# Attention logits on one core: the relative half in four quarter tiles of the array, with the first norm's steps moved among logits and transposes

## The chip, the cores and the metric

The kernel runs on one core of a Trainium2 chip. The metric is the device time of one execution in microseconds (us), the median of three runs. TensorE is called PE, VectorE DVE, ScalarE ACT, GpSimd POOL and SyncE, which issues DMAs, SP, as in the profile.

## The reference

64 images become 64 patch tokens each by a linear layer, a class token and 128 text tokens are joined to them: L = 193 tokens of 128 channels. Then comes attention with group norms and relative position terms, and a mixture of experts with 8 experts of 512, both as residuals. What the change touches is the attention:

```
qkv = group_norm(layernorm(h) @ W_qkv)          # 8 heads; q, k of 8 channels, v of 16
rel_idx = arange(L)[:, None] - arange(L)[None, :] + (L - 1)
rpe = rel_emb[:, rel_idx]                       # rpe_q, rpe_k (8 rows each), rpe_v (16)
logits = einsum('bhdi,bhdj->bhij', q, k) \
       + einsum('bhdi,dij->bhij', q, rpe_k) + einsum('bhdi,dij->bhij', k, rpe_q)
attn = softmax(logits)
out = einsum('bhij,bhdj->bhdi', attn, v) + einsum('bhij,dij->bhdi', attn, rpe_v)
h = h + group_norm(out);  h = h + ffn(layernorm(h))
```

In the mixture each token's two best gates multiply its input, every expert's dense layer is computed for both, gelu is applied to each and the two are summed before the second layer.

## The kernel before, in words

A first phase (`patch_embed`) makes the patch tokens. Then `fused_block` works on pairs of batch items, 32 pairs; channels lie on the 128 partitions, the 2 x 193 = 386 tokens of a pair along the free side. Each engine has its own instruction stream, written by hand: all go through the same list `SCHEDULE`, and for each name in it every engine issues its part of that step, in order. Engines meet through counting semaphores. One passage of the list is a turn. In a turn the MLP of pair n (32 chunks `c` or `a`, one per 128 of the 4096 hidden units) alternates with the attention of pair n+1, and the names in `EARLY` belong to the first half of the attention of pair n+2 (`txt` to `gaff`). There are 30 such turns in a loop, one more behind it with no early part, one ahead of it without MLP and one at the end with MLP alone.

A chunk (`mlp`): PE makes z in three matmuls of 386 columns into one of two banks (L429, L430, L433), VectorE multiplies z by a ratio (L607), ScalarE applies gelu to z in the bank (L817) and to the product (L818), GpSimd adds both (L889, issued two chunks later), and PE multiplies by the second layer's weights three chunks later (L420). A chunk's z waits for the first gelu of the chunk two before it, since it reads the same bank.

The attention of a pair:
- `txt`, `mean1`, `var1`, `bc1`, `proj`: transposes of the text, first layer norm (matmuls with a matrix of ones for sums and broadcasts, vector operations between, a power on GpSimd), projection to q, k, v. `gmean`, `gvar`, `gaff`: group norm of q, k, v by small matmuls and operations on 4 elements per partition; three of them on VectorE (`group_affine`, L650 to L654), then four scalings on ScalarE (L837, L840).
- SP writes q and k to DRAM and reads them back 8 times over into `a_rep`. `am0` to `am3` on VectorE multiply `a_rep` by a mask into `a_bd` (L700); `qs0` to `qs4` on GpSimd multiply q by a mask into `q_bd` (L918). So both hold block diagonal weights for blocks ("octs") of 8 queries times 16 (item, head) pairs: 25 octs.
- `log0` to `log12`: two octs each. PE: q_bd with k (L517), then a_bd with the relative rows `rw` (L518), added in the same bank, 193 columns each. The contraction of L518 has 128 rows: 16 source rows times 8 queries. Every fp32 matmul call is two instructions in the trace. Four banks are used in turn. VectorE takes the maxima (L710), ScalarE the exp (L858) into `lp`.
- `tr0` to `tr6`: transposes of four octs each into two banks, copied by VectorE (L715) and ScalarE (L864). `rel0` to `rel6`: product with the relative rows of v (L561, L562), masked by VectorE into `wm`, which lies in lp (L723).
- `pv0`, `pv1`: products with v and with ones, four column tiles of 32 at once (L543); `rec0`, `rec1`: reciprocals (L659); `place0`, `place1`: the relative part added to the banks, in the same tiles (L571), then normalised and measured for the next group norm by VectorE (L732 to L737).
- `omean`, `ovar`, `oaff`, `oh2`, `mean2`, `var2`, `bc2`, `gate`, `gate2`, `bcast`: output group norm, residual (L750), second layer norm, gates.

## Time and profile before

| | us |
|---|---|
| median of 3 runs | 3425.13 (3424.44 to 3427.97) |
| profiled execution, its own time | 3423.42 |
| its span | 3421.6 |

| engine | busy us | share of span | instructions |
|---|---|---|---|
| PE (matmul) | 3200.4 | 94% | 21952 |
| DVE | 1981.0 | 58% | 4052 |
| ACT | 1832.8 | 54% | 3570 |
| POOL | 1447.1 | 42% | 1350 |

The busy times are those of one profiled execution. A share is an average over the span; what bounds a stage is read from the timeline of that stage, where a bracket behind a row gives how long the engine stood idle and which instruction released it. Matmuls are pipelined, so the times of two rows overlap, and the distance from start to start is what one costs. PE's granted clock is 0.99 of full speed in the mean of the span.

### The profile page before, as it was taken

Reading aid. Unit: us, or ns where it says so; the run is one execution under the profiler, and the core shown is the slowest. Engines: PE = TensorE matmul, PEld = TensorE weight load, DVE = VectorE, ACT = ScalarE, POOL = GpSimd, SP = SyncE. Lnnn points to the kernel's source line nnn. Section 1 sums busy time; section 2 is a strip of 40 time slices with the busy share of each in tenths; the row PEclk is TensorE's granted clock in tenths of the full one; section 3 lists DMA queues with packets and bytes.
Section 4 is the critical chain, followed back from the end, with each engine's and each line's share of the span. In section 5 each row is a group of like instructions: output and inputs, shape, how many; then the busy total and the mean of one; then the engine's idle time right before and its main releaser. Section 6 shows DMA issues by size and latency. Waiting matters only on the chain.

```text
span 3421.6 us, 65186 instructions
## 1 busy us (share of the span) xinstructions
PE 3200.4 (94%) x21952; PEld 2602.3 (76%) x21952; DVE 1981.0 (58%) x4052; ACT 1832.8 (54%) x3570; POOL 1447.1 (42%) x1350
## 2 busy tenths in 40 slices
PE   7977999999999999999999999999999999999998
PEld 5867777777777777777777777777777777777776
DVE  4644655566565556665555566655555666655554
ACT  4632555555555555555555555555555555555556
POOL 1010444455434444554444445544444555344446
PEclk9987999999999999999999999999999999999999
DMA  9961001111110011111101111111011111100110
GB/s 202 219 179 30 14 16 26 24 26 26 26 24 9 22 24 26 26 26 26 24 7 24 24 26 26 26 26 24 5 26 24 26 26 26 26 23 6 24 25 5
DMA packets 92174, 121.41 MB, mean 35 GB/s; under 512 B 8414, under 2 KB 86558, under 8 KB 87710
## 3 DMA queue, kind: packets, MB, share of 16 engines
q1 hardware_dynamic: 87714, 118.24, 14.9%
q10 hardware_dynamic: 4432, 2.79, 0.3%
q8 instruction: 17, 0.28, 0.0%
q14 instruction: 11, 0.09, 0.0%
HBM read 106.04 MB, written 14.97 MB: 35 GB/s over the span
## 4 chain that ended last, share of the span: by engine, by line
issue 39%; PE 25%; POOL 15%; DVE 9%; ACT 4%; DMA 0%; DVEq 0%; POOLq 0%; ACTq 0%; SPq 0%
POOL gelu L889 10%; PE bank L420 7%; POOL q_bd L918 4%; PE bank L461 4%; PE bank L429 3%; DVE gelu L607 3%; PE bank L433 2%; DVE dl L760 2%; PE bank L430 2%; ACT gelu L817 2%; DVE gst L650 1%; PE bank L493 1%; POOL rs L902 1%; ACT e L840 1%; PE bank L449 1%
## 5 line engine op out<-in xcount | busy, mean ns | idle before, releaser
L889 POOL TENSOR_TENSOR gelu<-gelu 128x386 f32<-128x386 f32 x1024 | 1068.3, 1055 | 1477.9 <-ACT gelu L818 1474.7
L817 ACT ACTIVATE gelu<-bank,b_s 128x386 f32<-128x386 f32 x1024 | 595.2, 581 | 878.2 <-DVE gelu L607 867.0
L420 PE MATMUL bank<-gelu,w_s 128*128 128x386 f32 x2048 | 834.8, 494 | 45.6 <-POOL gelu L889 41.4
L607 DVE TENSOR_TENSOR gelu<-bank,ratio 128x386 f32<-128x386 f32 x1024 | 565.1, 557 | 476.4 <-PE bank L433 470.7
L818 ACT ACTIVATE gelu<-gelu,b_s 128x386 f32<-128x386 f32 x1024 | 624.3, 610 | 0.0
L429 PE MATMUL bank<-x_hi,w_hi 128*128 128x386 f32 x1024 | 524.6, 512 | 78.0 <-ACT gelu L817 73.8
L420 PEld LDWEIGHTS bank<-gelu,w_s 128*128 128x128 f32 x2048 | 361.6, 189 | 105.6 <-POOL gelu L889 87.0
L517 PE MATMUL bank<-k_f,q_bd 128*128 128x193 f32 x1600 | 393.6, 328 | 8.2 <-DVE a_bd L700 8.2
L518 PE MATMUL bank<-rw,a_bd 128*128 128x193 f32 x1600 | 393.2, 328 | 0.0
L858 ACT ACTIVATE lp<-bank,mx 128x193 f32<-128x193 f32 x800 | 288.0, 419 | 195.5 <-DVE mx L710 194.3
L429 PEld LDWEIGHTS bank<-x_hi,w_hi 128*128 128x128 f32 x1024 | 193.9, 189 | 253.7 <-ACT gelu L817 176.6
L710 DVE TENSOR_REDUCE mx<-bank 128x2 f32<-128x386 f32 (+1 forms) x416 | 225.1, 541 | 259.8 <-PE bank L518 255.9
L433 PE MATMUL bank<-x_lo,w_hi 128*128 128x386 f32 x1024 | 347.2, 339 | 0.0
L430 PE MATMUL bank<-x_hi,w_lo 128*128 128x386 f32 x1024 | 347.1, 339 | 0.0
L561 PE MATMUL bank<-probs,rv 128*128 128x128 f32 x1600 | 309.1, 274 | 0.0
L562 PE MATMUL bank<-probs,rv 65*128 65x128 f32 x1600 | 309.1, 274 | 0.0
L723 DVE TENSOR_TENSOR lp<-bank,con 128x512 f32<-128x512 f32 (+1 forms) x224 | 139.0, 633 | 284.4 <-PE bank L562 284.4
L517 PEld LDWEIGHTS bank<-k_f,q_bd 128*128 128x128 f32 x1600 | 281.9, 191 | 8.6 <-issue 8.6
L518 PEld LDWEIGHTS bank<-rw,a_bd 128*128 128x128 f32 x1600 | 283.6, 191 | 0.0
L562 PEld LDWEIGHTS bank<-probs,rv 65*128 65x128 f32 x1600 | 242.2, 191 | 0.0
L561 PEld LDWEIGHTS bank<-probs,rv 128*128 128x128 f32 x1600 | 241.8, 191 | 0.0
L530 PE MATMUL bank<-con,lp 128*128 128x128 f32 (+1 forms) x1600 | 220.8, 275 | 17.6 <-ACT lp L858 10.5
(131 smaller groups left out, 4266.6 us busy)
## 6 DMA issues: line engine op xcount, KB each, us to landing
a_rep<-u_scratch SPq DMA_DIRECT2D x32, 1600.0 KB, 9.8
xt<-in_x SPq DMA_DIRECT2D x192, 196.0 KB
txt_s<-in_txt SPq DMA_DIRECT2D x32, 128.0 KB, 2.2
u_scratch<-k_f SPq DMA_DIRECT2D x32, 100.0 KB, 2.2
u_scratch<-q_f SPq DMA_DIRECT2D x32, 100.0 KB, 2.2
out<-o_s SPq DMA_DIRECT2D x64, 48.5 KB
out<-o_s SPq DMA_DIRECT2D x64, 48.0 KB
rv<-in_rel_v SPq DMA_DIRECT2D x1, 2624.0 KB, 14.0
```

The source lines that it names most:

```text
L420: mm(yb[:, 0:T2], w2_s[:, f, :], gelu1[:, f % RING, :], start=(f == 0), stop=(f == NF - 1)).then_inc(S["w2_done"], 1)
L429: mm(z, w1_hi[:, w], x_hi[:, :], start=True, stop=False)
L430: mm(z, w1_lo[:, w], x_hi[:, :], start=False, stop=False)
L433: mm(z, w1_hi[:, w], x_lo[:, :], start=False, stop=True).then_inc(S["z_ready"], 1)
L517: mm(dst, q_bd[:, o, :, :], k_f[:, 0:L], start=True, stop=False)
L518: m = mm(dst, a_bd[:, o, :, :], rw[:, 192 - 8 * o:192 - 8 * o + L], start=False, stop=True)
L561: mm(part, rv[:, (8 * o + P) * HD:(8 * o + P) * HD + P], pr[0][:, o, :, :], start=True, stop=False)
L562: m = mm(part, rv[0:JC[1][1], 8 * o * HD:8 * o * HD + P], pr[1][0:JC[1][1], o, :, :], start=False, stop=True)
L607: v.tensor_tensor(gelu2[:, f % RING, :], zb[f % 2][:, 0:T2], ratio[:, :], ALU.mult).then_inc(S["z2_done"], 1)
L817: a(gelu1[:, f % RING, :], zb[f % 2][:, 0:T2], ACT.Gelu, bias=b1_s[:, f:f + 1]).then_inc(S["g_done"], 1)
L818: a(gelu2[:, f % RING, :], gelu2[:, f % RING, :], ACT.Gelu, bias=b1_s[:, f:f + 1]).then_inc(S["g_done"], 1)
L889: g.tensor_tensor(gelu1[:, f % RING, :], gelu1[:, f % RING, :], gelu2[:, f % RING, :], ALU.add).then_inc(S["hs_done"], 1)
```

## The change

It has four parts.

1. The relative half of the logits. The mask blocks become groups of 4 queries: `q_bd`, `a_bd` and `probs` go from [P, 25, 16, 8] to [P, 50, 16, 4]. `a_rep` holds the 16 source rows 4 times in each half of the partitions, filled by two DMAs of half the size instead of one. For an oct o the two groups g of 4 queries are computed with 64 rows (partitions 0 to 63 for even o, 64 to 127 for odd o) and 64 columns (64 g), so that four such calls have four different quarters of the array. `rw` is laid out to match.
2. A logits step has four octs in two banks; two sets of two banks alternate, so there are 7 steps instead of 13, and PE waits for the exps of the step before last. Even octs go to the first bank of a set, odd ones to the second. The q half stays as it was in the array. The first transpose waits for the last but one step, whole.
3. Mask pieces: `AM` is (0, 6, 12, 20, 25) octs, `QS` (0, 4, 12, 20, 25), one piece fewer, and am1 and qs1 stand ahead of the first logits step, the others about two steps ahead of their use.
4. The order. The early steps of the next pair move: txt, mean1 and var1 between the logits steps, bc1 behind tr1, proj behind rel6, gmean, gvar and gaff among pv, place and their chunks. Three chunks `c` stand ahead of am0 instead of four, and six instead of seven ahead of the logits; another one stands between place0 and place1.

The rows of `lp` become 196 long instead of 193, `wm` keeps whole rows, and the mask for it has full rows. The diff, cut to its core:

```diff
-RW = 2 * L - 1
+RW = 2 * L + 3
...
 SCHEDULE = (
-    "c c c c am0 c qs0 c c vt hkeep log0 am1 log1 qs1 log2 am2 log3 qs2 log4 log5 am3 log6 qs3 log7 log8 "
-    "qs4 log9 log10 log11 log12 tr0 tr1 rel0 c tr2 rel1 c tr3 rel2 tr4 rel3 tr5 rel4 tr6 rel5 rel6 "
-    "c pv0 c rec0 pv1 c rec1 place0 txt place1 c c omean mean1 c ovar c var1 oaff c bc1 oh2 c proj mean2 c "
-    "gmean c var2 gvar c bc2 c gaff c gate c c gate2 c c c c bcast w2t xin w2t w2t ot a otr a ocopy hres a"
+    "c c c am0 c qs0 c am1 c vt qs1 hkeep log0 log1 am2 qs2 log2 am3 log3 qs3 txt log4 mean1 log5 var1 log6 "
+    "tr0 tr1 bc1 rel0 c tr2 rel1 c tr3 rel2 tr4 rel3 tr5 rel4 tr6 rel5 rel6 "
+    "proj c pv0 c rec0 gmean pv1 c rec1 gvar place0 c place1 gaff c c omean c ovar c c oaff c oh2 c mean2 c var2 c c "
+    "bc2 c gate c c gate2 c c c c bcast w2t xin w2t w2t ot a otr a ocopy hres a"
 ).split()
...
-FILLS = (OCT + 1) // 2
-QS = (0, 5, 10, 15, 20, OCT)
-AM = (0, 7, 13, 19, OCT)
-LOGS = 4
+LGRP = 4
+LOGS = (OCT + LGRP - 1) // LGRP
+QS = (0, 4, 12, 20, OCT)
+AM = (0, 6, 12, 20, OCT)
...
-        lp = sb("lp", [P, OCT, L])
-        pr = [sb(f"probs{c}", [P, OCT, BH, 8]) for c in range(2)]
+        lp = sb("lp", [P, OCT, 196])
+        pr = [sb(f"probs{c}", [P, 2 * OCT, BH, 4]) for c in range(2)]
...
-                sp.dma_start(a_rep[:, :, :], u_scratch[:, :, :, :].rearrange("s d b i -> (s d) (b i)").unsqueeze(1)
-                             .broadcast_to([2 * DK, 8, BH * LP])).then_inc(S["a_spread"], 16)
+                for half in range(2):
+                    sp.dma_start(a_rep[64 * half:64 * half + 64, :, :], u_scratch[:, :, :, :].rearrange("s d b i -> (s d) (b i)").unsqueeze(1)
+                                 .broadcast_to([2 * DK, 4, BH * LP])).then_inc(S["a_spread"], 16)
...
-                    if i >= LOGS:
-                        pe.wait_ge(S["log_done"], t * FILLS + i - LOGS + 1)
-                    for k in range(2 if 2 * i + 1 < OCT else 1):
-                        o = 2 * i + k
-                        dst = lt[(i + 2) % LOGS][:, k * 256:k * 256 + L]
-                        mm(dst, q_bd[:, o, :, :], k_f[:, 0:L], start=True, stop=False)
-                        m = mm(dst, a_bd[:, o, :, :], rw[:, 192 - 8 * o:192 - 8 * o + L], start=False, stop=True)
+                    if i >= 2:
+                        pe.wait_ge(S["log_done"], t * LOGS + i - 1)
+                    octs = range(LGRP * i, min(OCT, LGRP * i + LGRP))
+                    place = lambda o: lt[2 * ((i + 1) % 2) + o % 2][:, o // 2 % 2 * 256:o // 2 % 2 * 256 + L]
+                    for o in octs:
+                        mm(place(o), q_bd[:, 2 * o:2 * o + 2, :, :], k_f[:, 0:L], start=(o // 2 % 2 == 0), stop=False, skip_group_check=True)
+                    for o in octs:
+                        row = 64 * (o % 2)
+                        for g in range(2):
+                            x0 = 196 - 8 * o - 4 * g
+                            m = mm(place(o)[64 * g:64 * g + 64, :], a_bd[row:row + 64, 2 * o + g, :, :],
+                                   rw[row:row + 64, x0:x0 + L], start=False, stop=True, skip_group_check=True,
+                                   tile_position=(row, 64 * g))
                     m.then_inc(S["log_ready"], 1)
...
                         if g == 0:
-                            pe.wait_ge(S["log_done"], t * FILLS + FILLS - 2 + c)
+                            pe.wait_ge(S["log_done"], t * LOGS + LOGS - 1)
...
-                    v.tensor_tensor(a_bd[:, o0:o1, :, :],
-                                    a_rep[:, :, 8 * o0:8 * o1].rearrange("p b (o r) -> p o b r", r=8),
-                                    K["mask_q"].unsqueeze(1).unsqueeze(1).broadcast_to([P, o1 - o0, BH, 8]),
+                    v.tensor_tensor(a_bd[:, 2 * o0:2 * o1, :, :],
+                                    a_rep[:, :, 8 * o0:8 * o1].rearrange("p b (o r) -> p o b r", r=4),
+                                    K["mask_q"].unsqueeze(1).unsqueeze(1).broadcast_to([P, 2 * (o1 - o0), BH, 4]),
                                     ALU.mult).then_inc(S["a_masked"], 1)
...
-                    act.wait_ge(S["max_done"], t * FILLS + i + 1)
-                    for k in range(w):
-                        o = 2 * i + k
-                        m = a(lp[:, o, 0:L], lt[(i + 2) % LOGS][:, k * 256:k * 256 + L], ACT.Exp, bias=mx[:, o:o + 1])
+                    for k in range(2 if LGRP * i + 1 < OCT else 1):
+                        act.wait_ge(S["max_done"], t * (2 * LOGS - 1) + 2 * i + k + 1)
+                        for z in range(2 if LGRP * i + 2 < OCT else 1):
+                            o, col = LGRP * i + k + 2 * z, LGRP * i + 2 * k + z
+                            m = a(lp[:, o, 0:L], lt[2 * ((i + 1) % 2) + k][:, z * 256:z * 256 + L], ACT.Exp, bias=mx[:, col:col + 1])
                     m.then_inc(S["log_done"], 1)
```

## Rows read from the trace of the kernel before

**Rows 1.** Busy time of each engine by stage of one turn, 1510.7 to 1608.8, and sum.
```profile
core 0: us, PE busy (x) PEld busy (x) DVE busy (x) ACT busy (x) POOL busy (x), PEclk, DMA share, GB/s
...
1527.00:1543.40 16.40, 16.40 (x103) 16.38 (x102) 9.73 (x15) 10.42 (x28) 8.11 (x6) 1.00 0.00 0
...
sum 98.10, PE 93.37 PEld 75.53 DVE 57.99 ACT 53.50 POOL 44.98; mean PE 18.67 PEld 15.11 DVE 11.60 ACT 10.70 POOL 9.00
```

**Rows 2.** PE's timeline, logits and first transposes (start, us, engine, line, idle before).
```profile
1527.05 0.49 PE L517 MATMUL bank<-k_f,q_bd 128*128 128x193 f32 x2
...
1543.38 0.60 PE L530 MATMUL bank<-con,lp 128*128 128x128 f32 x4
1544.31 1.11 PE L530 MATMUL bank<-con,lp 128*65 128x128 f32 x8 [0.33 <-ACT lp L858]
1545.64 0.65 PE L530 MATMUL bank<-con,lp 128*65 128x128 f32 x4 [0.22 <-ACT probs L864]
```

**Rows 3.** PE's timeline, single places of the same turn.
```profile
1525.86 0.92 PE L420 MATMUL bank<-gelu,w_s 128*128 128x386 f32 x2 [0.77 <-POOL gelu L889]
...
1579.81 0.28 PE L580 MATMUL bank<-gst_o,con 128*128 128x2 f32 x2
...
1580.56 0.81 PE L420 MATMUL bank<-gelu,w_s 128*128 128x386 f32 x2
1581.20 0.77 PE L455 MATMUL bank<-con,e 128*97 128x1 f32 x8
...
1594.77 0.92 PE L420 MATMUL bank<-gelu,w_s 128*128 128x386 f32 x2 [0.27 <-POOL gelu L889]
...
1599.34 0.44 PE L429 MATMUL bank<-x_hi,w_hi 128*128 128x386 f32 x1 [0.60 <-ACT gelu L817]
```

**Rows 4.** PE's timeline, product with v in column tiles and its neighbours.
```profile
1570.93 0.52 PE L543 MATMUL bank<-probs,v_pad 65*32 65x200 f32 x8
1571.27 0.52 PE L543 MATMUL bank<-probs,one_pad 65*32 65x200 f32 x8
1571.72 0.44 PE L429 MATMUL bank<-x_hi,w_hi 128*128 128x386 f32 x1
...
1572.35 0.81 PE L420 MATMUL bank<-gelu,w_s 128*128 128x386 f32 x2
1573.09 0.94 PE L571 MATMUL bank<-lp,con 128*32 128x200 f32 x16
```

**Rows 5.** ScalarE's timeline of that turn.
```profile
1533.78 1.36 ACT L858 ACTIVATE lp<-bank,mx 128x193 f32<-128x193 f32 x4 [1.29 <-DVE mx L710]
...
1597.10 0.51 ACT L837 ACTIVATE q_f<-bank,gst 128x193 f32<-128x193 f32 x1 [0.88 <-DVE gst L654]
...
1598.70 0.59 ACT L817 ACTIVATE gelu<-bank,b_s 128x386 f32<-128x386 f32 x1
```

**Rows 6.** VectorE's timeline of that turn.
```profile
1531.65 1.63 DVE L700 TENSOR_TENSOR a_bd<-a_rep,con 128x768 f32<-128x768 f32 x1
...
1535.57 0.95 DVE L700 TENSOR_TENSOR a_bd<-a_rep,con 128x768 f32<-128x768 f32 x1
...
1541.62 0.56 DVE L710 TENSOR_REDUCE mx<-bank 128x2 f32<-128x386 f32 x1 [0.75 <-PE bank L518]
...
1544.02 0.69 DVE L715 COPY probs<-bank 128x512 f32<-128x512 f32 x1
...
1573.03 1.36 DVE L659 RECIPROCAL t<-bank 128x193 f32<-128x193 f32 x1
...
1575.04 0.18 DVE L737 BATCH_NORM_AGGREGATE mv_o<-st_o 128x2 f32<-128x6 f32 x1
...
1584.97 0.76 DVE L750 TENSOR_TENSOR h<-h,t 128x193 f32<-128x193 f32 x2
...
1595.01 1.66 DVE L650 TENSOR_TENSOR gst<-vec,gst 128x4 f32<-128x4 f32 x1
```

**Rows 7.** GpSimd's timeline of that turn.
```profile
1521.83 1.77 POOL L889 TENSOR_TENSOR gelu<-gelu 128x386 f32<-128x386 f32 x1 [0.16 <-ACT gelu L818]
1523.56 1.29 POOL L918 TENSOR_TENSOR q_bd<-q_f,con 128x640 f32<-128x640 f32 x1
...
1593.70 2.94 POOL L889 TENSOR_TENSOR gelu<-gelu 128x386 f32<-128x386 f32 x3
```

65 lines of the change are left out of this document (33 added, 32 removed).

## The prediction

> **What bounds the kernel now.** I first read the table of busy time by stage of one steady turn [rows 1]: TensorE (PE) works 93.4 of 98.1 us. The turn, in which MLP chunks and the attention of the next pair alternate, comes 31 times at nearly the same length, so the change is worth 31 times what it does to one turn. Then I read PE's timeline for the places where it stands still. The logits run from 1527.05 to 1543.38 without a gap, 50 calls of 0.327 us [rows 2]. Behind them PE stands 0.33 us for an exp and 0.22 us for a copy of transposed probabilities. Of its other stops three matter here: 0.77 us before the logits, because GpSimd's sum is late, and in the long second half 0.27 and 0.60 us [rows 3]. So PE's work counts in full, and anything that makes a small chain late shows at once.
>
> **PE work removed.** The relative half is 25 of the 50 calls, 25 x 0.327 = 8.17 us. After the change it is 50 calls of 64 rows by 64 columns, in the order (row 0, column 0), (0, 64), (64, 0), (64, 64): one round of four calls per two blocks of eight queries, 2 rounds in a full step of four blocks and 1 in the last, so 13. The trace has no row tiles. The nearest is the product with v in four column tiles: 8 instructions (four calls) start every 0.34 us with 200 columns [rows 4], where one call alone takes about that, so four streams go at once. Lower bound of a round: 0.327 + 0.01 = 0.33 us, if the two row halves run together as the columns do. Upper bound: only the column pair does, 0.66 us. I take 0.33, since the column case is the nearest row and even and odd blocks write different banks: 13 x 0.33 = 4.29, a gain of 3.88 us.
>
> **Changes of array mode.** Each step now goes from the full array to tiles and back. Two full-array instructions of the MLP are followed by the next full-array one after 0.64 us (1580.56 to 1581.20 [rows 3]), but by the tiled one after 0.74 us (1572.35 to 1573.09): 0.09 to 0.10 us to go in. The last tiled round starts at 1571.27 and would end its turn at 1571.61, the next full instruction starts at 1571.72: 0.11 us to come out [rows 4]. Seven steps x 0.20 = 1.41 us. Net PE work: -3.88 + 1.41 = -2.47 us per turn. Chunks, transposes, products with v and the first norm's own matmuls are the same in number. The one chunk now between place0 and place1 costs the same out and in as txt did there.
>
> **The logits' pipeline.** A step is 4 x 0.327 + 2 x 0.33 + 0.20 = 2.17 us for PE. Its two banks come free when VectorE has reduced the first (start 0.2 us after PE, 0.56 us [rows 6]) and ScalarE has done four exps (1.36 us [rows 5]): with two hand-overs of 0.03 to 0.06 us, 2.21 us after the step. The step after next waits for that, having had 2.17 us: 0.04 us, nothing. But the third mask piece (1024 elements) stands on VectorE between the reductions of steps 1 and 2. 768 elements took 0.95 us alone and 1.63 us beside GpSimd's work [rows 6], so it takes 1.2 to 2.1 us where about 1.1 are free; step 4 then waits 0 to 0.63 us. I take 0.35. The query spread has pieces of 4 and 8 blocks; by 1.29 us for 5 [rows 7], 8 take some 2.1 to 2.3, just inside step 0's 2.17 us. The fourth mask piece and the vector operations of txt and mean1 fit, because mean1's matmul (two instructions of 386 columns, 0.64) makes step 5 late anyway.
>
> **Into the transposes.** tr0 needs step 5's exps, 2.21 us after that step. In between PE has var1 (eight instructions, 0.77 with the overlap of the last [rows 3], 0.62 to the next start) and the last step (2 x 0.327/2 + 0.33 + 0.20 = 0.87): a stop of 0.72 us. The copy of tr0 on VectorE ends 0.2 + 0.69 us [rows 6] after tr0's first half, while PE has another 0.44 of work, tr0's second half: 0.50 more. Against 0.33 + 0.22 today [rows 2] that is +0.67 us. bc1 does not help, it comes behind tr1.
>
> **Ahead of the logits.** The mask piece am0 made a GpSimd sum take 1.77 us where three others take 2.94 together, and with the query piece (1.29) behind it gave PE's 0.77 us stop [rows 3, 7]. Now two mask pieces (0.95 each) stand there, but qs0 has 4 blocks and one chunk fewer is there. Bounds -0.2 (shorter qs0) and +0.5 (am1 holds GpSimd up as am0 does); I take +0.1.
>
> **The group norm's affine, moved to right behind place1.** This is the largest charge. I count from place0's start. rec1 on VectorE (1.36 us, started 0.06 us before place0 today [rows 6]; gvar's matmul makes that 0.2) ends at 1.1; gvar's small add follows, GpSimd's power lasts from 1.3 to 2.3, if it takes what a sum does; place0's three operations (0.83 us from the end of rec1 to 1575.22) end at 2.2, then chunk A's multiply. PE: place0 0.87, A till 2.15, place1 till 3.1, B (inputs of its multiply at 3.9) till 4.4, C till 5.6, omean, and at 5.7 it wants D, whose bank must have been read by B's first gelu. VectorE: place1's operations end at 4.1, then the affine's three small ones. A chunk is 1.28 us of PE (1571.72 to 1573.09 [rows 4] without the 0.09), its multiply's input is there 0.8 in. GpSimd, held at the power, then has the sums of three chunks without a pause, from 2.3 to 5.35. Today the first affine operation, four elements from SBUF with SBUF, lay on VectorE from 1595.01 to 1596.67 and ended with a row of three sums (1593.70 to 1596.64) [rows 6, 7]. If that repeats, the affine ends at 5.75; without it, at 4.65. ScalarE then does q, k and v (1597.10 to 1598.70 today, 1.6 us [rows 5]) ahead of B's gelu (0.59). D starts at 8.05 or 6.95: a stop of 2.35 or 1.25 us. I take 2.35, as that is what the row shows for this instruction in this situation. Today's 0.60 us stop has the same cause, and the 0.27 us is a late sum behind two powers, one of which moves [rows 3]: -0.87. Net +1.48, lower bound +0.38.
>
> The Trainium skill, "SBUF — State Buffer", section "Who interferes with whom", says that a VectorE instruction with two SBUF inputs contends with GpSimd's reads, and that the winner of the shared ports holds them for the whole instruction. The row agrees that there is contention, but the wait passed over the end of a sum at about 1595.7, so it was longer than one instruction. If the page's unit of one instruction held, the affine would be free at 4.36 and the stop would be about 1.4 us and the sum -0.4 per turn, 3412 us: inside rival 1, and its chance is part of that rival's.
>
> **The second norm's chain.** Between ovar and mean2 PE now has four chunks, some 4.8 us. Today the chain of small steps from ovar's matmul (1579.81 [rows 3]) to the end of the two additions (1585.73 [rows 6]) lasts 5.9 us, hidden under three chunks and the first norm's matmuls; part of it is waiting behind that norm's vector operations, which are gone. Bounds 0 and 1.1 us of waiting; I take 0.25. Before var2 one chunk (1.2) stands against two vector operations of 386 columns (0.56 each as the reduction of as many) and hand-overs: 0.15. In all 0.4, bounds 0.15 and 0.9. DMA: the replicated source goes in two halves of the same bytes, asked for earlier against a need only slightly earlier; nothing.
>
> **The sum.** -2.47 + 0.35 + 0.67 + 0.1 + 1.48 + 0.4 = +0.53 us per turn; x 31 = +16.4. The profiled span of 3421.6 becomes 3438.0; that execution took 3423.4 (1.8 more), and the median 3425.1 is another 1.7 higher: **3441 us**. With all lower bounds: -2.47 + 0 + 0.67 - 0.2 + 0.38 + 0.15 = -1.47, 3379 us. With all upper: +0.63 + 0.67 + 0.5 + 1.48 + 0.9 - 2.47 = +1.71, 3478 us.
>
> **Rivals.** (1) **The affine isn't held up**: faster. Only the 1.10 us changes: +0.53 - 1.10 = -0.57 per turn, 3407 us. It decides at the point where the affine ends before GpSimd's row of sums does (under about 5.2 us after place0). For it: today this operation began when a third sum was already queued, there the row of sums may end sooner; against it the 1.66 us [rows 6]. With a free mask piece and ahead part as well it is the 3379 above. (2) **The row halves don't run together.** Rounds of 0.66: +4.29, less the 0.35 that a longer step hides, +0.53: +4.5 per turn, 3563 us. For it: no row of this trace has row tiles. Against it: banks and partitions are kept apart just as the columns' are. The gain would then not exist at all, only the mode changes. (3) **Runs of four elements are read more slowly.** The probabilities are now laid out in runs of four instead of eight, read by the 16 rounds of 0.34 us of the products with v; at double time +5.4 and the sum's +0.53 per turn, 3609 us. Nothing in the trace shows such runs; runs of eight go at the full rate. (4) **It cancels**: chain waits take what the tiles give, 3425 us.
>
> **How the numbers follow.** Forecast case 0.37 (own range 3428 to 3478), rival 1 and its neighbours 0.38, cancelling 0.13, row halves 0.08, runs of four 0.04. A change below 0.2% (7 us) can't be told from none with this kernel. Faster 0.38, within 0.2% 0.13, slower 0.37 + 0.08 + 0.04 = 0.49. The range, from 3375 to 3490 us, leaves out the two expensive rivals (0.12) and a little on the fast side. As cases of both signs hold most of the chance, the likeliest one's own range is 3428 to 3478.
>
> **What would show it.** Right: the relative instructions start in clusters of four, one cluster every 0.17 us; logits with about 14 us of PE work; a stop before tr0 of 0.7 us; and a stop of over 2 us at the second chunk after place1, released by ScalarE's gelu, while the affine's first operation lies over a row of sums. Wrong: the relative instructions one after the other (rival 2), products with v over 0.34 us per round (rival 3), or a short affine (rival 1). The prediction fails most easily on the waits of the second half, which are worked out from an order of instructions, not read.

## The result, and the profile after

| | before | after |
|---|---|---|
| median | 3425.51 us (3424.44 to 3427.97) | 3477.51 us (3474.60 to 3481.22) |
| span of the profiled execution | 3421.6 us | 3474.0 us |
| mean turn, from logits to logits | 98.07 us | 99.68 us |

The ratio is 1.0152, with a 95% interval of 1.0136 to 1.0168: the change makes the kernel slower by 52 us. The forecast was slower by 16 us, inside a range that went to 3490. The direction and most mechanisms hold; the size does not, and what follows is mostly about where the other 36 us lie. The medians are of all runs of a kernel and the ratios of its fast runs alone; the only slow run of this document is one of the four of e2_tiles (3512.5 us).

First, where in the span the 52.4 us between the two profiled executions are. From the first logits step on there are 31 turns. Thirty of them are longer by 1.61 us each: 48.3. The time up to the first logits step grows from 261.6 to 266.4 (+4.8), the first turn is shorter by 4.2, and what follows the last logits step is longer by 3.5. So the matter is decided in the steady turn. The table of busy time for a typical one of after (1546.12 to 1645.58; columns as in [rows 1]: stretch, length, busy time of PE, PE's weight loads, VectorE, ScalarE, GpSimd, each with its number of instructions, then granted clock, DMA share, GB/s):

```profile
1546.12:1645.58 99.46, 91.39 (x710) 70.89 (x709) 55.77 (x125) 53.32 (x110) 43.67 (x42) 1.00 0.09 23
```

PE is busy for 91.4 us of 99.5. Before, it was busy for 93.4 of 98.1 [rows 1]. PE's busy time has fallen by 2.0 us, as intended, and its idle time has risen by 3.3, from 4.7 to 8.1.

PE's timeline shows the logits (start, length, line, operation, tiles, count, and in brackets the idle time ahead of the row with what ended it). L519 is the q half in the full array, L524 the relative half in quarters; L451 is mean1, L457 var1, L538 the transposes, L422 and L431 chunks of the MLP:

```profile
1544.93 0.92 PE L422 MATMUL bank<-gelu,w_s 128*128 128x386 f32 x2 [1.25 <-POOL gelu L898]
1545.68 0.60 PE L471 MATMUL bank<-con,e 128*128 128x128 f32 x4
1546.12 1.47 PE L519 MATMUL bank<-k_f,q_bd 128*128 128x193 f32 x8
1547.52 0.89 PE L524 MATMUL bank<-rw,a_bd 64*64 64x193 f32 x16
1548.34 1.58 PE L519 MATMUL bank<-k_f,q_bd 128*128 128x193 f32 x8
1549.84 0.88 PE L524 MATMUL bank<-rw,a_bd 64*64 64x193 f32 x16
1550.65 1.57 PE L519 MATMUL bank<-k_f,q_bd 128*128 128x193 f32 x8
1552.16 0.89 PE L524 MATMUL bank<-rw,a_bd 64*64 64x193 f32 x16
1553.19 1.57 PE L519 MATMUL bank<-k_f,q_bd 128*128 128x193 f32 x8
...
1557.99 0.92 PE L451 MATMUL bank<-h,con 128*128 128x386 f32 x2
1558.74 1.47 PE L519 MATMUL bank<-k_f,q_bd 128*128 128x193 f32 x8
1560.14 0.88 PE L524 MATMUL bank<-rw,a_bd 64*64 64x193 f32 x16
1560.96 0.85 PE L457 MATMUL bank<-con,e 128*97 128x1 f32 x8
1561.67 0.57 PE L519 MATMUL bank<-k_f,q_bd 128*128 128x193 f32 x2
...
1563.10 1.09 PE L538 MATMUL bank<-con,lp 128*128 128x128 f32 x8 [0.39 <-ACT lp L867]
1564.54 1.09 PE L538 MATMUL bank<-con,lp 128*128 128x128 f32 x8 [0.35 <-DVE probs L724]
```

A full step is 2.31 to 2.32 us from start to start (1548.34 to 1550.65, 1547.52 to 1549.84), where 2.17 was forecast. The 16 instructions of its relative half start within 0.55 us in clusters of four, as this answer for a window of half a microsecond shows (duration least/median/most, then first and last start): twelve instructions of 0.32 us in a stretch of 0.4.

```profile
L524 PE MATMUL bank<-rw,a_bd x12: 322/323/375, 1547.5 to 1547.9; 64*64 64x193 f32 x12
```

So the quarters do run four at once. Without mean1 (0.75 us), var1 (0.71) and txt (0.28), which now stand between the steps, the logits take 14.85 us (1546.12 to 1562.71) against 16.33 before [rows 2]. That difference of 1.48 is not yet PE's work. The fourth step starts at 1553.19, which is 2.54 us after the third and 0.22 later than a full step would let it: it waited for the third mask piece on VectorE, which ends at 1552.96.

```profile
1551.74 1.22 DVE L708 TENSOR_TENSOR a_bd<-a_rep,con 128x1024 f32<-128x1024 f32 x1
```

And mean1, var1 and txt, each of which now stands behind a stretch of tiles, take some 0.1 us more here than behind full-array work (mean1 0.75 against the 0.64 that the prediction has for it), which is cost of the tiles too.

PE's stops in the second half of the turn, against 0.27, 0.60 [rows 3] and 1.04 us before:

```profile
1603.26 0.44 PE L431 MATMUL bank<-x_hi,w_hi 128*128 128x386 f32 x1 [1.97 <-ACT gelu L826]
...
1606.84 0.92 PE L422 MATMUL bank<-gelu,w_s 128*128 128x386 f32 x2 [0.21 <-POOL gelu L898]
...
1611.17 0.92 PE L451 MATMUL bank<-h,con 128*128 128x386 f32 x2 [1.06 <-DVE h L759]
...
1616.52 0.92 PE L422 MATMUL bank<-gelu,w_s 128*128 128x386 f32 x2 [0.53 <-POOL gelu L898]
```

A stop of 0.95 us follows at 1622.88, then 0.53, 0.27 and 1.25 ahead of the logits, as 0.54, 0.26, 0.25 and 0.76 before. The 1.97 is the forecast stop at the chunk called D in the prediction (the third whose z PE makes behind place1; the prediction's last paragraph and the expectations say the second), the 1.06 lies ahead of mean2, the others are late sums. The causes stand on VectorE (both affines: L658, L660, L662, which were L650 to L654) and on GpSimd (L911 a power, L898 the sums of chunks):

```profile
1599.58 0.23 DVE L658 TENSOR_TENSOR gst<-vec,gst 128x4 f32<-128x4 f32 x1
1599.84 0.94 DVE L660 TENSOR_TENSOR gst<-gst 128x4 f32<-128x4 f32 x1
1600.81 0.16 DVE L662 TENSOR_TENSOR gst<-vec,gst 128x4 f32<-128x4 f32 x1
...
1607.14 0.63 DVE L658 TENSOR_TENSOR gst_o<-vec,gst_o 128x2 f32<-128x2 f32 x1
1607.80 0.93 DVE L660 TENSOR_TENSOR gst_o<-gst_o 128x2 f32<-128x2 f32 x1
1608.77 0.93 DVE L662 TENSOR_TENSOR gst_o<-vec,gst_o 128x2 f32<-128x2 f32 x1
```

```profile
1597.81 2.95 POOL L898 TENSOR_TENSOR gelu<-gelu 128x386 f32<-128x386 f32 x3
1603.79 1.01 POOL L898 TENSOR_TENSOR gelu<-gelu 128x386 f32<-128x386 f32 x1 [3.03 <-ACT gelu L827]
1605.09 0.71 POOL L911 TENSOR_TENSOR gst_o<-gst_o,half 128x2 f32<-128x2 f32 x1 [0.29 <-DVE gst_o L751]
1605.77 3.92 POOL L898 TENSOR_TENSOR gelu<-gelu 128x386 f32<-128x386 f32 x4
```

An operation on two or four elements takes 0.16 us when GpSimd rests and up to 0.94 beside its sums. The reader should lay the two tables over each other: the row of three sums has its ends at about 1598.8, 1599.8 and 1600.8, and the first affine's operations end at 1599.81, 1600.78 and 1600.97. The row of four has ends at about 1606.8, 1607.7, 1608.7 and 1609.7, and the second affine's end at 1607.77, 1608.73 and 1609.70. Five of the six end within 0.02 us of a sum's end, and the next sum has started by the time the next operation does, so a chain of three can cost three sums. The sixth, the last of the first affine, begins when the row of sums is over and takes 0.16 us.

### The profile page after: what moved, and what is told of

It is laid out like the page before. It is cut to its first block, busy times and chain, and to the rows that moved or that the text cites. A ratio compares the mean times of both kernels' runs of the same rounds, so it can differ in the third digit from the quotient of the medians.

```text
span 3474.0 us, 67572 instructions
## 1 busy us (share of the span) xinstructions
PE 3158.1 (91%) x23552; PEld 2470.5 (71%) x23552; DVE 1891.3 (54%) x4052; ACT 1826.9 (53%) x3570; POOL 1409.5 (41%) x1318
## 4 chain that ended last, share of the span: by engine, by line
PE 52%; POOL 15%; issue 15%; DVE 6%; ACT 4%; POOLq 0%; DMA 0%; ACTq 0%; SPq 0%; DVEq 0%
POOL gelu L898 14%; PE bank L519 8%; PE bank L422 7%; PE bank L551 5%; PE bank L569 5%; PE bank L570 5%; PE bank L538 5%; PE bank L524 5%; PE bank L431 3%; PE bank L435 2%; PE bank L432 2%; PE bank L579 2%; PE bank L495 1%; ACT gelu L826 1%; PE bank L463 1%
## 5 line engine op out<-in xcount | busy, mean ns | idle before, releaser
L898 POOL TENSOR_TENSOR gelu<-gelu 128x386 f32<-128x386 f32 x1024 | 1057.4, 1048 | 1038.5 <-ACT gelu L827 1037.9
L422 PE MATMUL bank<-gelu,w_s 128*128 128x386 f32 x2048 | 848.3, 501 | 92.0 <-POOL gelu L898 88.2
L431 PE MATMUL bank<-x_hi,w_hi 128*128 128x386 f32 x1024 | 559.3, 546 | 88.1 <-ACT gelu L826 83.8
L422 PEld LDWEIGHTS bank<-gelu,w_s 128*128 128x128 f32 x2048 | 369.9, 192 | 156.3 <-POOL gelu L898 139.7
L867 ACT ACTIVATE lp<-bank,mx 128x193 f32<-128x193 f32 x800 | 274.1, 424 | 206.6 <-DVE mx L719 203.3
L431 PEld LDWEIGHTS bank<-x_hi,w_hi 128*128 128x128 f32 x1024 | 196.9, 192 | 252.7 <-ACT gelu L826 153.0
L719 DVE TENSOR_REDUCE mx<-bank 128x2 f32<-128x386 f32 (+1 forms) x416 | 208.5, 540 | 272.7 <-PE bank L524 272.7
L911 POOL TENSOR_TENSOR rs<-rs,half 97x4 f32<-97x4 f32 x64 | 65.1, 1017 | 656.6 <-DVE rs L638 656.6
L519 PE MATMUL bank<-k_f,q_bd 128*128 128x193 f32 x1600 | 312.3, 336 | 13.9 <-DVE a_bd L708 8.4
L519 PEld LDWEIGHTS bank<-k_f,q_bd 128*128 128x128 f32 x1600 | 259.1, 191 | 52.6 <-ACT lp L867 25.4
L432 PEld LDWEIGHTS bank<-x_hi,w_lo 128*128 128x128 f32 x1024 | 198.0, 193 | 70.3 <-issue 2.5
L873 ACT ACTIVATE probs<-bank 65x512 f32<-65x512 f32 (+1 forms) x224 | 121.6, 543 | 228.3 <-PE bank L538 228.3
```

Of the source, the lines that this page charges most:

```text
L422: mm(yb[:, 0:T2], w2_s[:, f, :], gelu1[:, f % RING, :], start=(f == 0), stop=(f == NF - 1)).then_inc(S["w2_done"], 1)
L431: mm(z, w1_hi[:, w], x_hi[:, :], start=True, stop=False)
L432: mm(z, w1_lo[:, w], x_hi[:, :], start=False, stop=False)
L519: mm(place(o), q_bd[:, 2 * o:2 * o + 2, :, :], k_f[:, 0:L], start=(o // 2 % 2 == 0), stop=False, skip_group_check=True)
L867: m = a(lp[:, o, 0:L], lt[2 * ((i + 1) % 2) + k][:, z * 256:z * 256 + L], ACT.Exp, bias=mx[:, col:col + 1])
L898: g.tensor_tensor(gelu1[:, f % RING, :], gelu1[:, f % RING, :], gelu2[:, f % RING, :], ALU.add).then_inc(S["hs_done"], 1)
```

## The experiments

All kernels here compute the whole of the reference. "Turn" is the mean distance between the logits of two turns, from the profile, with 98.07 for before and 99.68 for after. "Turn at full clock" is the mean of those turns in which PE's granted clock never falls to half, and behind it stands how many of the 30 turns in the loop have such a fall; it is 98.07 (0) for before and 99.47 (13) for after. The kernel before had medians of 3423.8 to 3424.9 us in the three groups of runs, and each ratio is to the one of its own group.

| kernel | median us | ratio (95%) | turn us | turn at full clock |
|---|---|---|---|---|
| e1_order: before + the new order | 3514.16 | 1.0262 (1.0244 to 1.0279) | 101.17 | 100.68 (19) |
| e2_tiles: after with the old order of the norm | 3462.32 | 1.0105 (1.0085 to 1.0125) | 98.98 | 98.76 (4) |
| e3_gaff: after, gaff behind bc2 | 3458.31 | 1.0107 (1.0090 to 1.0124) | 99.01 | 99.01 (0) |
| e4_modes: after, changes of mode doubled | 3540.35 | 1.0339 (1.0321 to 1.0356) | 101.72 | 101.41 (18) |
| e5_oaff_act: second affine on ScalarE | 3472.04 | 1.0141 (1.0124 to 1.0158) | 99.58 | 99.08 (10) |
| e6_am2: e2 + am2 ahead of the logits | 3435.43 | 1.0030 (1.0018 to 1.0043) | 98.25 | 98.08 (3) |
| e7_mix: tiles + a third order | 3407.35 | 0.9949 (0.9932 to 0.9965) | 97.50 | 97.50 (0) |
| e9_hold: after, GpSimd waits for the first affine | 3444.80 | 1.0057 (1.0040 to 1.0074) | 98.60 | 98.60 (0) |
| e8_qs0: e7 + qs0 a turn earlier | 3377.35 | 0.9858 (0.9842 to 0.9875) | 96.50 | 96.50 (0) |
| e10_qs01: e8 + qs1 too | 3364.48 | 0.9828 (0.9807 to 0.9850) | 96.03 | 96.03 (0) |
| e11_serial: after, quarter by quarter | 3482.59 | 1.0168 (1.0147 to 1.0188) | 99.81 | 99.62 (14) |

**The two halves of the change alone.** e1_order keeps the full array and takes the order:

```diff
-    "c c c c am0 c qs0 c c vt hkeep log0 am1 log1 ...
-    "c pv0 c rec0 pv1 c rec1 place0 txt place1 c c omean mean1 c ovar c var1 oaff c bc1 oh2 c proj mean2 c "
+    "c c c am0 c qs0 c am1 c vt qs1 hkeep log0 log1 log2 log3 am2 qs2 log4 log5 am3 log6 qs3 log7 txt qs4 "
+    "log8 log9 mean1 log10 log11 var1 log12 tr0 tr1 bc1 rel0 ... rel6 proj c pv0 c rec0 gmean pv1 c rec1 gvar "
+    "place0 c place1 gaff c c omean c ovar c c oaff c oh2 c mean2 c var2 c c bc2 c gate ..."
```

> The kernel before with the new order alone: logits still 13 steps on the full array, first norm's steps among logits and transposes, gaff behind place1, am1 and qs1 ahead of the logits. Theory A (the order costs, the tiles gain): PE keeps all 50 full calls, the second half has its stops of about 2 us at the second chunk after place1 and about 1 us before mean2; +2.5 to +3 us per turn against before, some 3505 to 3515 us. Theory B (the steps of four octs and the mode changes cost, the order is harmless): within 10 us of before, 3425 us.

e2_tiles is after with the norm's steps where before has them, and four chunks ahead of am0:

```diff
-    "rec1 gvar place0 c place1 gaff c c omean c ovar c c oaff c oh2 c mean2 c var2 c c bc2 c gate c "
+    "rec1 place0 txt place1 c c omean mean1 c ovar c var1 oaff c bc1 oh2 c proj mean2 c gmean c var2 gvar c bc2 c gaff c gate c "
```

> The changed kernel with the old order of the first norm (txt to gaff where they stood, seven chunks ahead of the logits); tiles, steps of four octs and mask pieces as changed. Theory A: PE work 1.5 us less per turn, 0.7 to 1 us of new waits at the transposes and ahead of the logits: -0.5 us per turn, about 3410 us. Theory B: slower than before, 3450 us or more.

The order alone costs 3.10 us per turn, and the tiles on top of it give back 1.49 (101.17 to 99.68). At full clock it is 2.62 and 1.21; the rest are turns in which the clock falls, which the order alone has more of. e1 shows after's stops one for one: 1.86 us for a gelu behind place1, 1.07 ahead of mean2, 0.52 and 0.96 for late sums. That much was as expected. With the old order, however, the tiles did not give a gain but cost 0.91 (0.69 at full clock), and the first theory of e2 fails. VectorE's and PE's timelines of e2 say why:

```profile
1556.58 2.11 DVE L708 TENSOR_TENSOR a_bd<-a_rep,con 128x1024 f32<-128x1024 f32 x1
```

```profile
1558.93 1.57 PE L519 MATMUL bank<-k_f,q_bd 128*128 128x193 f32 x8 [1.04 <-DVE a_bd L708]
1568.02 1.09 PE L538 MATMUL bank<-con,lp 128*128 128x128 f32 x8 [1.08 <-ACT lp L867]
```

The third mask piece lay beside two of GpSimd's sums and took 2.11 us, so the fourth step waited 1.04. And with nothing of the norm between the last steps, tr0 waits 1.08 us for the exps of the last but one step: PE had saved time that the pipeline behind it did not give.

**e6_am2** moves the third mask piece ahead of the logits:

```diff
-    "c c c c am0 c qs0 c am1 c vt qs1 hkeep log0 log1 am2 qs2 log2 am3 ...
+    "c c c c am0 c qs0 c am1 c vt am2 qs1 hkeep log0 log1 qs2 log2 am3 ...
```

> The kernel e2_tiles with one mask piece (am2) moved from behind log1 to ahead of the logits. Theory: its 2.11 us beside GpSimd's sums were the stop of 1.04 us at log3; the stop goes, at most 0.3 us comes back at log1 because GpSimd's query piece is held up instead: -0.7 us per turn, about 98.2 us per turn. Rival: the exps set the pace and a stop of the same size appears at another step; turn within 0.2 us of e2_tiles' 99.0.

As expected: the stop at the fourth step is gone, 0.35 us for a piece of q_bd comes at the second, and the turn is 98.25 (98.08 at full clock, as before). So with the old order the tiles are worth nothing even with that stop gone: of the PE time saved, tr0's stop takes 0.74 (1.07 for 0.33) and the stop ahead of the logits 0.5 (1.25 for 0.76).

**The largest stop.** e3_gaff takes gaff to behind bc2:

```diff
-    "... place0 c place1 gaff c c omean c ovar c c oaff c oh2 c mean2 c var2 c c bc2 c gate c "
+    "... place0 c place1 c c omean c ovar c c oaff c oh2 c mean2 c var2 c c bc2 gaff c gate c "
```

> The changed kernel with only gaff moved from behind place1 to behind bc2. Theory A: the stop of 1.97 us at the second chunk after place1 goes, a stop of about 0.6 us like the old one comes at the gate: -1.4 us per turn, about 3435 us. Rival: the stop only moves, because the output norm's chain is what is late: within 10 us of the changed kernel, 3477 us.

The 1.97 us stop goes, but the turn falls by 0.67 only where 1.4 was expected, and 0.20 of that is the clock. Up to mean2 PE is 1.8 us earlier in the turn than in after (mean2 63.3 us behind the first logits step instead of 65.1), and behind bc2 it loses 1.3 us again. The stop ahead of mean2 stays at 1.06, so gaff was not its cause; at bc2's end a late sum costs 0.43 and a gelu 0.24 where neither was, and the turns that were longer than the typical one are typical again. e9_hold leaves the order alone and keeps GpSimd away from the affine: at gaff GpSimd waits for its end before it takes further sums.

```diff
+                elif s == "gaff":
+                    pool.wait_ge(S["affine"], t + 1)
```

> The changed kernel with one more wait on GpSimd: the two sums behind gaff don't begin before VectorE's three small operations of the q, k, v affine are done. Theory C: these then take 0.5 us instead of 1.4, the stop of 1.97 us at the second chunk after place1 falls by 0.8 to 1.0, but the sums come later and PE stops 0.3 to 0.6 us at a product with a late sum: -0.3 us per turn, about 3465 us. Rival (no contention, the affine is late for its inputs): stop unchanged, and slower by the late sums, 3485 us.

```profile
1592.68 0.13 DVE L658 TENSOR_TENSOR gst<-vec,gst 128x4 f32<-128x4 f32 x1
1592.84 0.16 DVE L660 TENSOR_TENSOR gst<-gst 128x4 f32<-128x4 f32 x1
1593.04 0.16 DVE L662 TENSOR_TENSOR gst<-vec,gst 128x4 f32<-128x4 f32 x1
```

```profile
1594.41 0.92 PE L422 MATMUL bank<-gelu,w_s 128*128 128x386 f32 x2 [0.79 <-POOL gelu L898]
```

The three operations take 0.52 us from the first start to the last end instead of 1.39, PE's stop for the gelu is gone, and one of 0.79 for the delayed sum stands in its place, more than the 0.3 to 0.6 expected. The turn falls by 1.08 us (0.87 at full clock), where 0.3 was expected. This is the direct proof of what makes the first affine long: the same operations at the same place in the order, with GpSimd at rest, are short.

**The stop ahead of mean2.** e5_oaff_act computes the output norm's affine on ScalarE, which doesn't take part in the contention:

```diff
-                    group_affine(2, gst_o, S["orstd"], S["oaff_part"], S["oaffine"], ...)
+                    a(gst_o[:, 5, 0:2], gst_o[:, 4, 0:2], ACT.Identity, scale=OS).then_inc(S["oaff_part"], 1)
+                    ...
+                        a(gst_o[:, 2, b:b + 1], gst_o[:, 0, b:b + 1], ACT.Identity, scale=gst_o[:, 5, b:b + 1]).then_inc(S["oaff_part"], 1)
+                    ...
+                    a(gst_o[:, 6, 0:2], gst_o[:, 2, 0:2], ACT.Identity, bias=OB, scale=-1.0).then_inc(S["oaffine"], 1)
```

> The changed kernel with the output group norm's affine (three operations on two elements, which took 0.63, 0.93 and 0.93 us on VectorE beside a row of GpSimd's sums) done by four small operations of ScalarE instead, nothing else moved. Theory C (VectorE's small operations are held up by GpSimd's): the chain to mean2 gets some 1 to 1.5 us shorter, the stop of 1.06 us before mean2 falls under 0.3 us, -0.8 us per turn, about 3452 us. Rival (the chain is late because of the chunks queued in it): stop unchanged within 0.2 us, 3477 us, or more by the ScalarE time added.

A miss for the most part: the stop falls from 1.06 to 0.72, not below 0.3. ScalarE's timeline shows what is late now: the gelu of a chunk stands ahead of the affine until 1605.30, and its four instructions take 1.13 us by themselves.

```profile
1604.79 0.61 ACT L824 ACTIVATE gelu<-gelu,b_s 128x386 f32<-128x386 f32 x1
1605.30 0.28 ACT L874 ACTIVATE gst_o<-gst_o,vec 128x2 f32<-128x2 f32 x1
1605.62 0.48 ACT L877 ACTIVATE gst_o<-gst_o 128x1 f32<-128x1 f32 x2
1606.13 0.30 ACT L879 ACTIVATE gst_o<-gst_o,vec 128x2 f32<-128x2 f32 x1
```

The turn at full clock is 0.39 us shorter, which is about the 0.34 by which the stop fell; in the mean only 0.10 of it is left, since a turn in which the clock falls is 1.5 us longer here and 0.5 in after. So the contention is a part of that stop (0.34 us at least). The rest is, by the rows, a chain that needs some 6 us from ovar's matmul to h and has four chunks, 4.8 us, to hide under; no run separates that.

**The price of a change of mode.** e4_modes divides each step in two, with the q half and the relative half of two octs in turn; this makes six more times in and out per turn and changes nothing else:

```diff
-                    for o in octs:
-                        mm(place(o), q_bd[...] ...)
-                    for o in octs:
-                        ...
+                    for pair in (octs[0:2], octs[2:4]):
+                        for o in pair:
+                            mm(place(o), q_bd[...] ...)
+                        for o in pair:
+                            ...
```

> The changed kernel with each full logits step split into q of two octs, relative of two octs, twice: six more changes into tiles and back per turn, same matmuls. With the 0.36 us per pair of changes read from the changed kernel's trace (step 2.32 us against 2.61 us of the full array, two rounds of 0.33): +2.2 us per turn, some 3545 us. With the 0.20 us of the prediction: +1.2, some 3515 us. If a change costs nothing, 3477 us.

```profile
1576.40 0.56 PE L525 MATMUL bank<-rw,a_bd 64*64 64x193 f32 x8
1576.89 0.92 PE L520 MATMUL bank<-k_f,q_bd 128*128 128x193 f32 x4
1577.74 0.56 PE L525 MATMUL bank<-rw,a_bd 64*64 64x193 f32 x8
1578.23 0.92 PE L520 MATMUL bank<-k_f,q_bd 128*128 128x193 f32 x4
```

The turn grows by 2.04 us for six pairs of changes, 0.34 each, or by 1.94 at full clock, 0.32 each. The rows give nearly the same: two half steps of 1.34 us (1576.89 to 1578.23) against one of 2.32, 0.36. I had put 0.20.

**Do the quarters need an order?** e11_serial issues the calls of one column half before those of the other, two of the same quarter behind each other:

```diff
-                    for o in octs:
-                        row = 64 * (o % 2)
-                        for g in range(2):
+                    for g in range(2):
+                        for o in list(octs[0::2]) + list(octs[1::2]):
+                            row = 64 * (o % 2)
```

> The changed kernel with the relative calls of a step in another order of issue: the two calls of one quarter next to each other, then the next quarter; same calls, same changes of array mode. If PE starts calls strictly in the order of issue, a quarter's second call holds up the next quarter's first: a full step has about 13 instruction times of 0.163 us instead of 4, +1.4 us per full step, +8 to +9 us per turn, about 3740 us. If quarters have queues of their own, no change, 3477 us.

```profile
L524 PE MATMUL bank<-rw,a_bd x12: 323/323/374, 1551.1 to 1551.5; 64*64 64x193 f32 x12
```

The same twelve in 0.4 us, a turn of 99.81, 5 us in all above after, where a strict order of starts was expected to cost 8 to 9 us per turn. The order within a step matters by 0.14 us per turn at most: the second call of a quarter doesn't keep those of the other quarters from starting.

**Putting it together.** e7_mix takes the tiles, am2 ahead of the logits, and of the norm only what fills the gap ahead of tr0. txt, mean1, var1 and bc1 stay near logits and transposes; proj, gmean, gvar and gaff go back behind the output norm:

```diff
+    "c c c am0 c qs0 c am1 c vt am2 qs1 hkeep log0 log1 qs2 log2 am3 log3 qs3 log4 txt log5 mean1 log6 "
+    "tr0 var1 tr1 rel0 c tr2 bc1 rel1 c tr3 rel2 tr4 rel3 tr5 rel4 tr6 rel5 rel6 c pv0 c rec0 pv1 c rec1 "
+    "place0 place1 c c omean c ovar c c oaff c oh2 c proj mean2 c gmean c var2 gvar c bc2 c gaff c gate c "
```

> Tiles with an order chosen by the stops seen: am2 ahead of the logits, txt, mean1, var1 and bc1 in the stops around the transposes, proj to gaff where they stood before, one chunk ahead of the logits moved behind. Theory: the stops at tr0 (1.08) and tr1 (0.35) are filled by 1.3 us of work, no stop behind place1, some 0.5 us at mean2: 97.5 us per turn, about 3410 us. Rival: the second norm's chain takes it all back (1 us or more at mean2): 98.2 us per turn or more, no gain over the kernel before.

97.50 us as expected, and the first kernel that is faster than before, by 0.5%. Whether the old layout with this order would be as fast wasn't run, so what of this gain needs the tiles is open. Its largest stops are 1.24 ahead of the logits, for a sum behind a piece of q_bd, and 1.04 after gate. e8_qs0 takes the first piece of q_bd out of that place: its q is known since gaff of the turn before, so it goes ahead of that turn's output steps.

```diff
-EARLY = "txt mean1 var1 bc1 proj gmean gvar gaff".split()
+EARLY = "txt mean1 var1 bc1 proj gmean gvar gaff qs0".split()
-    "c c c am0 c qs0 c am1 c vt am2 qs1 hkeep log0 log1 ...
+    "c c c am0 c c am1 c vt am2 qs1 hkeep log0 log1 ...
-    "c gate2 c c c c bcast w2t xin w2t w2t ot a otr a ocopy hres a "
+    "c gate2 c c c c bcast w2t xin w2t w2t qs0 ot a otr a ocopy hres a "
...
                             pool.wait_ge(S["log_ready"], t * LOGS)
+                            pool.wait_ge(S["ffn_in"], t * 2)
```

> e7_mix with the first query piece (qs0, 1.04 us of GpSimd) done a turn earlier, behind the output matmuls of the MLP, where GpSimd stands still for about 4 us. Theory: the stop of 1.24 us ahead of the logits falls to 0.2 to 0.4 us, nothing comes back: 96.6 us per turn, about 3380 us. Rival: GpSimd's first sum of the new pair comes later by as much and the stop only moves to the first chunks: 97.5 us per turn as e7_mix, 3407 us.

e10_qs01 does the same with the second piece (`qs0 qs1` in both places).

> e8_qs0 with the second query piece (eight blocks, 2.0 us) moved there too. The stop of 0.36 us at log1 (GpSimd's piece late) goes; but 3.1 us of GpSimd now lie ahead of the first sum where 4 us less the wait for x_lo are free, so a stop of up to 0.8 us may come at the third or fourth chunk. Between -0.3 and +0.5 us per turn against e8_qs0.

e8's turn is 96.50, with the stop ahead of the logits gone; against the expectation something comes back, since the stop at the second step for q_bd grows from 0.36 to 0.85 us. e10 has neither and a turn of 96.03. That is 0.47 less than e8, more than the expected range of -0.3 to +0.5 had; the stop of up to 0.8 us at an early chunk is there, but has grown only from 0.25 to 0.53. Its table of busy time, with PE at 91.3 of 96.0, the same work as after's 91.4:

```profile
1500.40:1596.44 96.04, 91.26 (x711) 70.45 (x710) 59.66 (x126) 52.99 (x111) 44.74 (x42) 1.00 0.10 23
```

So e10 beats both kernels, 1.7% below before. Its qs pieces would help the old layout too, perhaps; that wasn't run, so the 1.7% is not a measure of the tiles.

## Why the prediction was right or wrong

Per turn the sum was +0.53 us; the typical turn is longer by 1.41 and the mean one by 1.61. By the steps of the prediction, the differences of starts in the two traces give the following. The first line leaves out the 0.22 us that the fourth step waited and counts with it the 0.1 us that txt, mean1 and var1 each take longer behind tiles:

| step | forecast | found | off by |
|---|---|---|---|
| PE work of the logits, with changes of mode | -2.47 | -1.4 | +1.05 |
| third mask piece | +0.35 | +0.2 | -0.15 |
| into the transposes | +0.67 | 0.0 | -0.67 |
| ahead of the logits | +0.1 | +0.35 | +0.25 |
| second half: gaff (1.48) and second norm (0.4) | +1.88 | +2.3 | +0.4 |
| sum | +0.53 | +1.4 | +0.87 |

**PE work: right mechanism, the mode term mis-sized.** The rounds of four quarters take 0.33 us, as taken from the column tiles [rows 4]; rival 2 (row halves one after the other) is out, and so is rival 3: the products with v still start a round every 0.34 us with runs of four elements. The step that failed is "seven steps x 0.20 = 1.41". It was read as the distance between the last instruction of one mode and the first of the other. The trace of after has that distance about as forecast, 0.09 in and 0.11 out. But the first instruction behind a change is itself slower: the first cluster of quarters lasts 0.21 us where the next take 0.165, and the first full instruction 0.27 where the next take 0.16. In all 0.36 by the rows and 0.34 by e4, 0.32 at full clock. So the term put at 1.41 us per turn measures 2.4 to 2.5. Seven times 0.15 is 1.05 us per turn, 33 us over the kernel, as much as nearly the whole of the missing 36; the errors of the other terms nearly cancel each other (-0.15, -0.67, +0.25, +0.4), which is luck. The distance from a stretch's first instruction in one mode to the same place in the next one is what had to be measured; the trace of before held it only for chunks beside place and pv [rows 4].

Of the missing 36 us some 26 are the typical turn's 0.87, some 6 the turns in which the clock falls and some 4 lie outside the thirty turns.

The Trainium skill says in "TensorEngine Tiling (Array Packing)", section "Key Properties", that a change of tiling mode drains TensorE. The runs agree in so far as a change in and out costs 0.32 to 0.36 us; that it is a drain they don't show. Its other sentence there, that tiles work independently of each other, is what e11's pace bears out.

**Third mask piece: right.** The fourth step waited 0.22 us for it, inside the bounds of 0 to 0.63. GpSimd's work on q_bd (5.04 us from 1545.80 to 1550.84) was done before the piece began, so it took 1.22 us from 1551.74, the lower end of "1.2 to 2.1". In e2, with another chunk ahead, the same piece met two sums and took 2.11, the upper end. The bounds were right and which of them holds is a matter of half a microsecond of alignment.

**Transposes.** The two stops were forecast as 0.72 + 0.50 and are 0.39 + 0.35, as stops 0.19 more than before's 0.33 + 0.22 [rows 2], and nothing from start to start. A likely reason, which no run here separates: the last steps, var1 and mean1 gave PE more work ahead of tr0 than I had counted, since each step has a dearer change of mode. A part of the error of the first line comes back here.

**Ahead of the logits.** +0.35 is inside the bounds of -0.2 and +0.5. The cause named for the upper one stands in the trace: a sum beside a mask piece takes 1.64 us, and the query piece comes before the next two sums (2.68). The stop is 1.25 us with one chunk fewer.

```profile
1540.55 1.64 POOL L898 TENSOR_TENSOR gelu<-gelu 128x386 f32<-128x386 f32 x1 [0.25 <-ACT gelu L827]
1542.16 1.04 POOL L927 TENSOR_TENSOR q_bd<-q_f,con 128x512 f32<-128x512 f32 x1
1543.17 2.68 POOL L898 TENSOR_TENSOR gelu<-gelu 128x386 f32<-128x386 f32 x2
```

**gaff behind place1: right.** The stop was forecast at 2.35 us, released by ScalarE's gelu, and is 1.97 with that releaser; the affine was to end 5.75 us after place0's start, and ends 1600.97 - 1595.53 = 5.44 after it, which accounts for most of the difference between the two stops. Rival 1 (the affine isn't held up) is out, and e9 shows the cause. How it is held up was put wrongly, however. I took one operation to be kept waiting by a whole row of sums, as 1.66 us in before seemed to say [rows 6]; here no operation waits longer than one sum, and it is the chain of three that waits several times. The Trainium skill, "SBUF — State Buffer", section "Who interferes with whom", gives the instruction as the unit of the lock. After's rows agree (0.94, 0.63, 0.93 and 0.93 us, each ending with a sum of 1.0). Before's 1.66 us still doesn't fit, and no run here explains it. The estimate that I made from that rule, a stop of 1.4, let only one operation be held up; the rule holds in after's rows and my use of it was wrong. With three sums in a row both readings give nearly the same end, so this term came out right partly by luck.

**Second norm's chain: mis-sized.** 0.25 us of waiting was forecast ahead of mean2 and 1.06 found, at the upper bound of 1.1. I argued that a part of the old 5.9 us was waiting behind the first norm and would go; but the second affine now lies beside a row of four sums and costs 2.56 us (1607.14 to 1609.70) by the very contention that I had charged to gaff. Before it took 1.30 us (1582.09 to 1583.39). How much of the stop this makes is shown only from below, 0.34 us by e5. The sum with all upper bounds was too low here as well: it took 0.9 for the whole of this term, whose first part alone had an upper bound of 1.1. I applied the reason to the operation that moved and not to the one that stayed while the sums around it moved. The late sums of 0.21 and 0.53 us are new, too, where I let the old 0.27 go.

**A loss that no step had.** Thirteen of after's turns are 0.3 to 1.4 us longer than the typical one. Each of them has one stretch in which PE's granted clock falls to half, beginning within 1.7 us of the end of the 1.97 us stop, and none of the other turns in the loop has one. Two stretches of such a turn, directly behind the 1.97 us stop (which ends at 1702.75); the third number from the right is the granted clock:

```profile
1703.70:1705.40 1.70, 1.70 (x8) 1.56 (x7) 0.60 (x2) 1.56 (x3) 1.39 (x3) 0.63 0.04 12
1705.40:1707.10 1.70, 1.70 (x5) 1.08 (x4) 0.56 (x1) 0.97 (x2) 1.70 (x2) 0.50 0.93 248
```

Half of full speed is the lower of the two levels, 1.2 GHz. The mean turn is 0.22 us above the typical one, some 7 us of the 52. With the stop gone (e3 and e9) no such turn is left: in e3 all but the first of the loop lie between 98.93 and 99.04 us. It isn't the length of 1.97 us that it takes. In e2 and e6 the clock falls behind the stop of 1.08 us ahead of tr0, in four and in three turns, and each of these is 1.6 us longer. A stretch of one in e2, whose stop ended at 2061.75:

```profile
2063.40:2065.10 1.70, 1.70 (x10) 1.70 (x10) 0.69 (x1) 0.07 (x1) 0.00 (x0) 0.50 0.00 0
```

Yet after's own stops of 1.06 and 1.25 us are never followed by such a fall. What decides in which turns the clock falls, these runs don't show.

**Outside the loop.** The 4.8 us up to the first logits step aren't settled: this part of the span, in which the images come in by DMA, took 261.6 us in before and 264.7 to 274.2 in the other kernels (274.2 in e2, 273.5 in e6, 266.8 in e10), and no run was made to tell what of that is the order and what the DMA.

**Chances and range.** 0.49 for slower was too modest a weight for what turned out clear, but the rivals on the fast side all leaned on the affine alone. The forecast's own upper sum was 3478 us, with every term at its upper end; the time came there by another road, one term (the mode) outside its bounds because it had none.

## What to carry to other kernels

Here small tiles would pay only for longer stretches in one mode: each time in and out costs 0.32 to 0.36 us with these fp32 calls, as much as one full-array call of 193 columns, so gather the calls of a mode before you divide the work. A chain of small VectorE operations with two SBUF inputs beside a busy GpSimd can cost one GpSimd instruction for each of them, so place it where GpSimd rests, or give GpSimd a wait. When a PE stage becomes shorter, look first at what was hidden under it: here the kernel with the tiles was no faster than before until the norm's steps filled the gap ahead of the transposes (e6 to e7: -0.75 us per turn, 0.16 of it the clock) and GpSimd's pieces were moved out of the way (e7 to e10: -1.47). And look whether the stops of PE, from 1 us here, are now and then followed by a fall of its clock, since such turns can hide or feign a gain (e5: 0.39 us per turn at full clock, 0.10 in the mean).

## What the runs showed of the hardware

- Four quarters of the array run at once, with 64 rows and 64 columns each: four fp32 calls of 193 columns in 0.33 us, as long as one takes in the full array. Two calls to the same quarter behind each other don't hold up the others by more than 0.14 us per turn (e11: 99.62 at full clock against 99.47). This was not expected: the Trainium skill says in "TensorE: Matmul & The Clock Gate", section "The mechanism", that matmuls start and end strictly in the order of the program, by which a pair in one quarter would have held up the rest. The trace gives the starts but not the quarter of each instruction, so this is read from the pace alone.
- The first instruction after a change of mode is longer than its successors, 0.05 us for the quarters and 0.10 for the full array.
- PE's granted clock fell to half behind some stops of PE of 1.08 us (e2, e6), 1.47 and 1.86 us (e1) and 1.97 us (after, e4, e5, e11), never in the loop of before, whose longest stop is 1.04. Such a turn is 0.3 to 1.7 us longer.
- A VectorE operation with few elements and both inputs in SBUF takes 0.13 to 0.16 us beside an idle GpSimd; beside a busy one most end with the sum in hand (up to 0.94 us), but one of before went on past it (1.66 us [rows 6]). Of the large ones, a mask piece of 1024 elements takes 1.22 us alone, 1.55 beside a part of a row (e6) and 2.11 beside two sums (e2).
- Two DMAs of 800 KB for `a_rep` land 7.6 us after their issue, one of 1600 KB after 9.8. VectorE waited for them only once in the whole kernel, ahead of the first logits (8.5 us, before 8.2), so nothing came of it.
